# Three small layers beside a biased attention layer: the next causal one runs before the last gated one, and the order of all steps is new

## The chip, the core and the metric

The kernel runs on one core of a Trainium2 chip. Its time is the device time of one launch in microseconds (us), the median of several runs. The core has a matrix engine (PE in the profile, with its weight loads shown as PEld), a vector engine (DVE), a scalar engine (ACT), a general engine (POOL), a queue engine (SP) that issues the transfers, and eight accumulation banks, the tile `ps`, into which PE writes and out of which DVE and ACT read.

## What is computed

The input x is 8 samples of 512 tokens by 256 channels, in float32. Four layers follow each other, each with its own normalisation and a residual sum:

```python
x = x + attn_a(layernorm(x))   # causal: 16 heads of 16, rotary positions
x = x + ffn(layernorm(x))      # gated, l = 1: top half of the tokens by a gate, attention among them, scattered back
x = x + attn_b(layernorm(x))   # biased: 16 heads of 64, a table of 511 relative biases, index clamped
x = x + ffn(layernorm(x))      # gated, l = 3: the same function and weights as l = 1
```

In the causal layer the scores are masked above the diagonal; in the gated layers 256 of the 512 tokens are chosen by the rank of their gate, and the result is weighted by the gate. Samples do not depend on each other.

## The kernel before

All work is cut into steps, `Step(kind, s, l, n, q)`: `s` is the sample, `l` the layer (0 causal, 1 gated, 2 biased, 3 gated), `n` a head group or a pair of heads, `q` a part of it. The letter ahead of a kind is that of its layer, `c_`, `f_` or `b_`. There are 2256 steps; 1760 of them run on PE. `Plan(whole())` makes one list of them, and each engine walks that one list and does its own share of each step, so that the list is the order on every engine at once. PE never overtakes: a PE step that waits holds up all behind it.

The list is made in `in_order`. Among the steps whose predecessors have been placed it takes the one with the smallest `turn`, a number that `turn` reads from the table `PLACE` by kind, `n` and `q`, in rows for the first samples (`first0`, `first1`, `first`), the repeated middle (`cycle`, `cycle3`) and the end (`last`, `last1`, `last2`); `CYCLE` times the sample is added in the middle. `whole()` gives the predecessors: the data that a step needs, and what must be placed ahead of it because memory is shared.

The program has this shape. Samples 0 and 1 start with their causal and first gated layers, with little to run beside them. Then come eight biased layers, one per sample, each of them the frame of a cycle: beside the biased layer of sample s run three small layers, and they run one after another in one shared place of memory (`side`, `place_of` 0): the last gated layer of sample s-1, then the causal layer of s+1, then the first gated layer of s+1. The last gated layer of sample 7 stands alone at the end. Cycles for s = 2 to 6 have the same order.

The steps that matter below:

- `b_k`, `b_q`, `b_v` are projections of a pair of heads (L960 in PE's rows), `b_row` a 128-row block of scores (L1691), `b_nrm` its division on POOL (L1133), `b_tr` its transposition (L1699), `b_val` its product with the values (L1709), `b_y` the output projection (L1470).
- `c_xt` transposes the normalised input (L1501), `c_q` and `c_k` project it (L960); DVE, POOL and ACT then rotate it and split it into a high and a low part (`c_dq`, `c_rq`, `c_xq`, `c_dk`, `c_hk`). `c_p1` (L1529) computes scores for the row maxima, which DVE takes (L1325); `c_p2` (L1553) computes them again, transposed and with the maximum taken off, and ACT takes their exponentials (L1198); `c_va` and `c_vb` are the products with the values.
- `f_q`, `f_k`, `f_v` are projections; `f_p1` (L1624) and `f_p2` (L1646) are the gated counterparts, read by DVE (L1399) and ACT (L1205). `f_hm` and `f_m` turn the maxima between them, `f_va` and `f_vb` (L1658) multiply with the values, `f_o` and `f_y` (L1470) end the layer.
- `c_p1`, `c_p2`, `f_p1` and `f_p2` each take four of the eight banks, and use PE in pieces of 32 rows. `b_row` uses 64 rows, `b_val` 64 columns, the value products of the small layers 32 columns, everything else the whole array. The column `32*128` or `128*64` in PE's rows is this cut.
- Where `in_order` expects PE to wait, it has idle transpositions put ahead of the step (L1490, `ps<-ident`), called fillers here: 653 matmuls in all. They compute nothing that is used.
- `load_rope` reloads two tables of 256 KB each (`cos`, `sin`) ahead of each causal layer, since a gated layer has overwritten them. SP issues it after the last `f_vb` of the gated layer that ran last in the place.

Of the kernel before, what the change touches and what calls it, by code (L numbers as in the profile page):

```python
# [187 lines left out]
def wait_for(x, y):  # L188
# [7 lines left out]
    if x.kind == "f_spread" and y.kind == "f_rank":  # L196
# [7 lines left out]
    ("cycle", "b_k"): [3518, 1169, 1334, 4006, 4463, -33303, 4684, 5254],  # L204
    ("cycle", "b_ln"): [-15605],
    ("cycle", "b_nrm"): [1730, 3640, 2810, 3176, -4032, 3806, 3306, 4094, 4046, 4157, 4200, 4231, -9958, 4064, -3484,
        -36992, 4582, -9960, 3649, 4846, -48934, 1082, -48936, 5309, -36527, 3182, 5174, 5565, -49123, 4685, 5627,
        5511],
    ("cycle", "b_q"): [1785, 979, -3985, 4186, -35860, -37112, 8, -13072],
    ("cycle", "b_row"): [3590, 761, 3095, 3597, -13675, 3728, 2692, 1528, 993, 4334, 4077, 3578, 4077, 4040, 3589,  # L210
        -9153, 4509, -35108, -9630, 4077, -35254, 5214, -32634, -12835, -37081, 5135, 3041, 5508, 5529, 5511, 5563,
        5383],
    ("cycle", "b_tr"): [3656, 3997, -9445, 4075, 3460, 4272, 4094, 3973, 4077, -34795, 4410, -37079, -9958, -9958,
        4065, 4504, 5008, 5131, 4114, -9717, -36997, 5317, -11276, 5429, 4877, 5442, 5681, -12901, 5249, 5696, 5264,
        4627],
    ("cycle", "b_v"): [2758, 3587, 4079, 4385, -71, 4805, -48961, -1478],
    ("cycle", "b_val"): [4352, -9978, 4104, 4067, -33729, 3381, 3714, 1132, 4591, -41659, -33412, 3315, -37187, 4670,
        4115, 3613, 5428, 3980, -9596, 4938, 5509, -1425, -32633, 5575, 5738, 5511, 5950, 5980, 6159, 4292, 6176,
        5511],
    ("cycle", "b_xt"): [3459],  # L220
    ("cycle", "b_y"): [6233, 6258, 5177, 6270],
    ("cycle", "c_dk"): [-1887, 1803],
    ("cycle", "c_dq"): [-7637, 1401],
    ("cycle", "c_hk"): [-38074, -40051],
    ("cycle", "c_hm"): [1885, 2367],
    ("cycle", "c_k"): [-10624, 1724],
    ("cycle", "c_ln"): [1401],
    ("cycle", "c_m"): [1174, -51742],
# [199 lines left out]
    ("last2", "f_spread"): [2866],  # L428
    ("last2", "f_v"): [22412],
    ("last2", "f_va"): [34817, 38087],  # L430
    ("last2", "f_vb"): [19123, 7896],
    ("last2", "f_xq"): [17183],
    ("last2", "f_y"): [41504, 5562],
}
# [1345 lines left out]
```

## Time and profile before

| what | value |
|---|---|
| median of 3 runs | 2064.11 us (2063.27 to 2064.46) |
| the profiled execution, whole | 2061.41 us |
| its span, first to last instruction | 2059.7 us |
| PE busy in the span | 1988.9 us (97%) |
| DVE, ACT, POOL busy | 1516.3, 1152.8, 692.5 us (74%, 56%, 34%) |
| transfers, 16 engines | 14.6% of their time, 50 GB/s |
| share of PE on the chain that ended last | 76% |

The page has the busy time of each engine and, in 40 slices of the span, the tenths of a slice in which it was busy. The timeline lists runs of equal instructions with their start; the distance from one row's start to the next row's start is what a step costs PE. PE's own durations overlap, since matmuls are pipelined. A matmul in plain float32 counts twice there.

### The profile page before, as it was taken

The page shows a single profiled execution, that of the slowest core. Times are in us where ns is not written, and L with a number is a line of the kernel's source. Part 1 is how long each engine was busy: PE and PEld are TensorE (multiplying, and loading weights), DVE is VectorE, ACT ScalarE, POOL GpSimd, SP SyncE. Part 2 cuts the span into 40 slices and gives each one's busy share as a digit, 9 for nine tenths or more (in the row PEclk, how much of TensorE's full clock was granted, in tenths as well). Part 3 has the DMA queues.
Part 4 walks back from the last instruction along what each step waited for, and adds up shares of the span by engine and source line. Part 5 has one row for each costly group of instructions (what it writes and reads, how often), then busy time and mean ns, then how long its engine had stood idle before and what let it go on. Part 6 is the DMA issues. An engine that isn't in the chain of part 4 may idle for free.

```text
span 2059.7 us, 42179 instructions
## 1 busy us (share of the span) xinstructions
PE 1988.9 (97%) x16097; PEld 1282.8 (62%) x16097; DVE 1516.3 (74%) x4803; ACT 1152.8 (56%) x2578; POOL 692.5 (34%) x879
## 2 busy tenths in 40 slices
PE   8999999999999999999999999999999999999998
PEld 6676666655666556765566655665566655675667
DVE  8977654967868767778778687686876967857446
ACT  2535764756637475374755657466573756627742
POOL 5323232343414433234423343234341343413320
PEclk9999999999999999999999999999999999999999
DMA  4001121120102211121111211012110120102200
GB/s 166 2 1 35 52 77 45 61 98 17 63 16 73 73 35 44 34 80 55 35 37 52 83 42 45 19 59 83 35 63 2 60 90 17 63 16 70 70 1 22
DMA packets 31079, 102.46 MB, mean 50 GB/s; under 512 B 3104, under 2 KB 11424, under 8 KB 30752
## 3 DMA queue, kind: packets, MB, share of 16 engines
q1 hardware_dynamic: 30880, 99.76, 14.6%
q8 instruction: 130, 2.13, 0.4%
q14 instruction: 69, 0.57, 0.1%
HBM read 95.56 MB, written 4.19 MB: 48 GB/s over the span
## 4 chain that ended last, share of the span: by engine, by line
PE 76%; DVE 12%; ACT 5%; POOL 3%; issue 2%; DVEq 0%; POOLq 0%
PE ps L960 18%; PE ps L1709 11%; PE ps L1691 11%; PE ps L1699 10%; PE ps L1470 9%; ACT PTc L1198 3%; PE ps L1553 3%; PE ps L1658 3%; PE ps L1646 3%; PE ps L1567 3%; DVE ps L1325 2%; PE ps L1529 2%; DVE peaks L1399 2%; DVE probs L1416 2%; PE ps L1624 1%
## 5 line engine op out<-in xcount | busy, mean ns | idle before, releaser
L1133 POOL TENSOR_SCALAR probs<-probs,rtotal 128x512 f32<-128x512 f32 x512 | 345.9, 695 | 513.2 <-DVE rtotal L1425 512.3
L1225 ACT ACTIVATE probs<-probs,peak 128x512 f32<-128x512 f32 x512 | 365.3, 715 | 134.2 <-DVE peak L1421 133.3
L1416 DVE CUSTOM_DVE_ANT_0 probs<-ps,band 128x512 f32<-128x512 f32 x512 | 332.7, 687 | 60.6 <-PE ps L1691 60.2
L1234 ACT ACTIVATE PT<-ps 128x512 f32<-128x512 f32 x512 | 261.5, 620 | 52.5 <-PE ps L1699 52.1
L1699 PE MATMUL ps<-ident,probs 128*128 128x128 f32 x2048 | 245.3, 274 | 3.6 <-DVE peaks L1399 2.2
L1325 DVE CUSTOM_DVE_ANT_0 ps<-ps,later 128x512 f32<-128x512 f32 (+3 forms) x512 | 232.6, 526 | 20.3 <-PE ps L1529 20.0
L1691 PE MATMUL ps<-KT,QT 64*128 64x512 f32 x1024 | 243.8, 607 | 0.0
L1699 PEld LDWEIGHTS ps<-ident,probs 128*128 128x128 f32 x2048 | 225.2, 141 | 29.2 <-POOL probs L1133 12.0
L1709 PE MATMUL ps<-PT,Vb 128*64 128x512 f32 x1024 | 237.0, 600 | 0.0
L960 PE MATMUL ps<-xnT,wb 128*128 128x512 f32 x512 | 233.4, 600 | 0.6 <-ACT xnT L1158 0.6
L1198 ACT ACTIVATE PTc<-ps 128x384 f32<-128x384 f32 (+1 forms) x384 | 168.2, 549 | 42.4 <-PE ps L1553 41.4
L1399 DVE TENSOR_REDUCE peaks<-ps 128x2 f32<-128x512 f32 x256 | 157.2, 682 | 22.2 <-PE ps L1624 22.2
L960 PEld LDWEIGHTS ps<-xnT,wb 128*128 128x128 f32 x512 | 93.6, 190 | 113.1 <-issue 107.0
L1125 POOL TENSOR_SCALAR_AFFINE_SELECT PTc<-PTc 128x512 f32<-128x512 f32 x128 | 81.5, 649 | 233.8 <-ACT PTc L1198 233.4
L1096 POOL TENSOR_TENSOR rstd<-veps,pow_half 128x2 f32<-128x2 f32 x64 | 46.5, 731 | 329.8 <-DVE veps L1256 329.8
L1691 PEld LDWEIGHTS ps<-KT,QT 64*128 64x128 f32 x1024 | 94.8, 186 | 91.6 <-issue 67.2
L1205 ACT ACTIVATE PTf<-ps 128x512 f32<-128x512 f32 x256 | 131.3, 646 | 34.0 <-PE ps L1646 34.0
L1709 PEld LDWEIGHTS ps<-PT,Vb 128*64 128x64 f32 x1024 | 66.6, 136 | 129.1 <-issue 117.0
L960 PEld LDWEIGHTS ps<-wb,xnT 128*128 128x128 f32 x1024 | 121.2, 192 | 24.6 <-issue 22.7
L960 PE MATMUL ps<-wb,xnT 128*128 128x128 f32 x1024 | 127.3, 278 | 0.0
L1470 PE MATMUL ps<-wob,OTb 128*128 128x256 f32 x512 | 113.7, 379 | 0.0
L1470 PEld LDWEIGHTS ps<-wob,OTb 128*128 128x128 f32 x512 | 96.6, 190 | 12.4
(156 smaller groups left out, 3343.0 us busy)
## 6 DMA issues: line engine op xcount, KB each, us to landing
band<-in_band SPq DMA_DIRECT2D x64, 896.0 KB, 4.6
wb<-in_w_b SPq DMA_DIRECT2D x64, 384.0 KB, 3.1
x<-in_x SPq DMA_DIRECT2D x16, 256.0 KB, 3.0
out<-x SPq DMA_DIRECT2D x16, 256.0 KB, 2.2
cos<-in_cos SPq DMA_DIRECT2D x8, 256.0 KB, 2.7
sin<-in_sin SPq DMA_DIRECT2D x8, 256.0 KB, 2.9
wob<-in_wo_b SPq DMA_DIRECT2D x1, 1024.0 KB, 8.6
wqk<-in_wqk_a SPq DMA_DIRECT2D x1, 512.0 KB, 5.8
```

The lines of the kernel that those rows point to most:

```text
L960: last = nc.tensor.matmul(o, w, r, start=(i == 0), stop=(i == len(pairs) - 1))
L1133: last = g.tensor_scalar(unit, unit, rtotal[:, r % 8, e:e + 1], 1.0, ALU.mult, ALU.mult)
L1198: a.activation(pt_c(m, q)[:, h], bank(now, name)[:, 0:w], ACT.Exp, scale=float(DH) ** -0.5).then_inc(act_read, 1)
L1225: last = a.activation(unit, unit, ACT.Exp, bias=peak[:, r % 8, e:e + 1], accum_out=total[:, r % 8, e:e + 1])
L1234: a.activation(PT[:, k % 2, e, :, tile_of(q)], bank(now, name).rearrange("p (k n) -> p k n", k=NT), ACT.Copy).then_inc(act_read, 1)
L1325: last = v.tensor_tensor_reduce(out=scores, in0=scores, in1=later[:, NT * P - w:NT * P], scale=1.0, scalar=-3e38, op0=ALU.add, op1=ALU.max ...
L1399: v.tensor_reduce(places[:, h:h + 1].rearrange("p h t -> p (h t)"), bank(now, name).rearrange("p (t n) -> p t n", t=NS), AXIS.X, ALU.max). ...
L1416: v.tensor_tensor_reduce(out=probs[:, r % ROWS_HELD, e, :], in0=bank(now, name), in1=band[:, k % 2, e, lo:lo + T], scale=1.0, scalar=-3e38 ...
L1470: last = te.matmul(o[:, j * D:(j + 1) * D], w, r, start=(k == 0 and j == 0), stop=(k == count - 1 and j == 1))
L1691: full(te.matmul(bank(now, name), QT2[half(e), k % 2, tile_of(q)], KT2[half(e), k % 2, :], start=True, stop=True), now, name)
L1699: last = te.transpose(bank(now, name)[:, tile_of(t)], probs[:, r % ROWS_HELD, e, tile_of(t)], ident[:])
L1709: last = te.matmul(o[half(e), :], Vb[:, k % 3, q, half(e)], PT[:, k % 2, e, q, :], start=(q == 0), stop=(q == NT - 1))
```

## The change

The three small layers beside a biased layer change places: first the causal layer of s+1, then the last gated layer of s-1, then the first gated layer of s+1. They still follow each other in the shared place. The condition for the rotary tables moves with it: they are reloaded after the last `f_vb` of the first gated layer, not of the last one. All numbers of `PLACE` are replaced, in the rows of the start and of the end too. No step is added or removed, and no operation of a step is changed.

```diff
@@ causal_steps
-    turned = [Step("f_vb", s - 2, 3, 1)] if s >= 2 else []
-    out = [(c("ln"), late, [Step("f_part", s - 2, 3)] if s >= 2 else []), (c("xt"), [c("ln")], side)]
+    turned = [Step("f_vb", s - 1, 1, 1)] if s >= 2 else []
+    out = [(c("ln"), late, [Step("f_part", s - 1, 1)] if s >= 2 else []), (c("xt"), [c("ln")], side)]
@@ whole
         if s > 0:
-            gone = add(ffn_steps(s - 1, 3), left, side)
-            side = gone
+            turned = []
             if s + 1 < B:
-                side = add(ffn_steps(s + 1, 1), add(causal_steps(s + 1, side), [], []), [])
+                turned = add(causal_steps(s + 1, side), [], [])
+            side = add(ffn_steps(s - 1, 3), left, turned + side)
+            if s + 1 < B:
+                side = add(ffn_steps(s + 1, 1), turned, side)
                 entered.append(side)
@@ block.sync
-                        if kind == "f_vb" and l == 3 and n == 1 and s + 2 < B:
+                        if kind == "f_vb" and l == 1 and n == 1 and 1 <= s < B - 1:
                             sp.wait_ge(heads_done, plan.after("heads", now, now))
-                            load_rope(sp, s + 2)
+                            load_rope(sp, s + 1)
@@ PLACE
-    ("cycle", "c_ln"): [1401],
...
-    ("cycle", "f_y"): [3437, 2898],
```

Lines after the table have numbers smaller by four in the changed kernel (L1470 is L1466 there, L1490 is L1486).

First place: PE, where a causal layer starts in a middle cycle. `xn` is the normalised input under transposition, `xnTc` the causal layer's transposed input, `xnT` the biased layer's, `wob` the weights of `b_y`. Before:

```order
L1470 MATMUL ps<-of_lo_143,spread_t_140 128x256 x2
L1501 MATMUL ps<-ident,xn 128x128 x8
L1490 MATMUL ps<-ident 128x128 x6
L960 MATMUL ps<-xnTc_106,wqk 128x512 x6
L960 MATMUL ps<-xnT,wb 128x512 x8
L960 MATMUL ps<-wb,xnT 128x128 x8
L1529 MATMUL ps<-LO_100,X_96 128x128 x4
```

Now:

```order
L1466 MATMUL ps<-of_lo_143,spread_t_140 128x256 x2
L1497 MATMUL ps<-ident,xn 128x128 x8
L1466 MATMUL ps<-wob,OTb 128x256 x8
L956 MATMUL ps<-xnTc_106,wqk 128x512 x2
L1497 MATMUL ps<-ident,xn 128x128 x8
L956 MATMUL ps<-xnTc_106,wqk 128x512 x6
L956 MATMUL ps<-xnT,wb 128x512 x4
L1466 MATMUL ps<-wob,OTb 128x256 x16
```

Six fillers stood between the transposition and the projections of the causal layer; now half of a `b_y` stands there, and the next biased layer's transposition lies between two of the projections. Behind the last projection of the causal layer nine steps of the biased layer follow before the first `c_p1` (2 `b_k`, 2 `b_q`, 2 parts of `b_y`, 3 `b_row`), where five projections of it did.

Second place: PE, in the last part of the first gated layer of a middle cycle (the rows of L1646 are one `f_p2` in two halves, then come the value products with `PTf` and `Vx`). Before:

```order
L1646 MATMUL ps<-gX_123,gLO_125 128x256 x4
L1646 MATMUL ps<-gX_123,gHI_124 128x256 x4
L1646 MATMUL ps<-gM_127,sel 128x256 x4
L1709 MATMUL ps<-PT,Vb 64x512 x4
L1658 MATMUL ps<-PTf_129,Vx 32x256 x16
L1709 MATMUL ps<-PT,Vb 64x512 x4
L1470 MATMUL ps<-wof,OTf_139 128x256 x4
```

Now:

```order
L1642 MATMUL ps<-gX_123,gLO_125 128x256 x4
L1642 MATMUL ps<-gX_123,gHI_124 128x256 x4
L1642 MATMUL ps<-gM_127,sel 128x256 x4
L1654 MATMUL ps<-PTf_129,Vx 32x256 x8
L1486 MATMUL ps<-ident 128x128 x5
L1654 MATMUL ps<-PTf_129,Vx 32x256 x8
L1705 MATMUL ps<-PT,Vb 64x512 x4
L1466 MATMUL ps<-wof,OTf_139 128x256 x4
```

Half of a `b_val` between the last `f_p2` and the value products is gone from there; five fillers have come between the two value products.

Third place: PE, in the same layer, from its projections to its first `f_p1` (L1624). Before:

```order
L1709 MATMUL ps<-PT,Vb 64x512 x2
L960 MATMUL ps<-xgT_141,wkf 128x256 x4
L960 MATMUL ps<-xgT_141,wqf 128x256 x4
L960 MATMUL ps<-wvf,xgT_141 128x256 x4
L1699 MATMUL ps<-ident,probs 128x128 x24
L1624 MATMUL ps<-gLO_125,gX_123 128x256 x4
```

Now:

```order
L956 MATMUL ps<-xgT_141,wqf 128x256 x4
L956 MATMUL ps<-xgT_141,wkf 128x256 x4
L956 MATMUL ps<-wvf,xgT_141 128x256 x4
L1695 MATMUL ps<-ident,probs 128x128 x32
L1620 MATMUL ps<-gLO_125,gX_123 128x256 x4
L1620 MATMUL ps<-gHI_124,gX_123 128x256 x4
```

One more `b_tr` (8 transpositions) stands between, and the projection of q comes ahead of that of k.

## Rows read from the trace of the kernel before

**Rows 1.** The page: busy time by engine, and PE and its clock in 40 slices.

```profile
PE 1988.9 (97%) x16097; PEld 1282.8 (62%) x16097; DVE 1516.3 (74%) x4803; ACT 1152.8 (56%) x2578; POOL 692.5 (34%) x879
...
PE   8999999999999999999999999999999999999998
...
PEclk9999999999999999999999999999999999999999
```

**Rows 2.** Busy time by stretch: the start, one middle cycle, the end; columns in the first line.

```profile
core 0: us, PE busy (x) PEld busy (x) DVE busy (x) ACT busy (x) POOL busy (x), PEclk, DMA share, GB/s
0.00:180.00 180.00, 164.86 (x1747) 116.30 (x1748) 151.31 (x495) 71.64 (x148) 66.31 (x83) 1.00 0.14 49
...
840.10:1087.20 247.10, 239.75 (x1940) 151.95 (x1939) 188.59 (x601) 143.93 (x322) 86.33 (x108) 1.00 0.15 50
...
1832.60:2059.70 227.10, 216.75 (x1616) 147.75 (x1614) 132.08 (x390) 115.53 (x262) 56.43 (x75) 1.00 0.12 40
```

**Rows 3.** The fillers alone (L1490), same stretches: length, PE busy, PEld busy.

```profile
0.00:180.00 180.00, 50.50 (x382) 41.41 (x382) 1.00 0.14 49
...
840.10:1087.20 247.10, 1.58 (x11) 1.21 (x11) 1.00 0.15 50
...
1832.60:2059.70 227.10, 24.99 (x199) 21.95 (x199) 1.00 0.12 40
```

**Rows 4.** Timeline of PE at the start: start, length, instruction, idle before.

```profile
start us, us, engine line op out<-in xcount [idle before <-releaser]
...
101.13 6.33 PE L1490 MATMUL ps<-ident 128*128 128x128 f32 x56
108.45 0.65 PE L1580 MATMUL ps<-ident,gate 128*128 128x128 f32 x4 [1.00 <-DVE gate L1364]
108.94 3.44 PE L1490 MATMUL ps<-ident 128*128 128x128 f32 x30
114.06 0.18 PE L960 MATMUL ps<-ones,tie 128*128 128x1 bf16 x1 [1.68 <-DVE above L1374]
```

**Rows 5.** Timeline of PE: a run of eight b_val parts.

```profile
905.85 7.09 PE L1709 MATMUL ps<-PT,Vb 128*64 128x512 f32 x32
912.87 1.97 PE L1699 MATMUL ps<-ident,probs 128*128 128x128 f32 x16
```

**Rows 6.** Timeline of PE: a single b_val part between two other cuts.

```profile
1058.89 1.08 PE L1709 MATMUL ps<-PT,Vb 128*64 128x512 f32 x4
1059.90 0.39 PE L1646 MATMUL ps<-gX,gLO 32*128 32x256 f32 x4
```

**Rows 7.** Timeline of PE where the causal layer of a middle cycle starts.

```profile
926.58 1.03 PE L1501 MATMUL ps<-ident,xn 128*128 128x128 f32 x8
927.45 0.82 PE L1490 MATMUL ps<-ident 128*128 128x128 f32 x6
928.57 5.42 PE L960 MATMUL ps<-xnTc,wqk 128*128 128x512 f32 x12 [0.30 <-ACT xnTc L1158]
...
943.52 0.33 PE L1529 MATMUL ps<-LO,X 32*128 32x128 f32 x4 [0.88 <-POOL LO L1118]
```

**Rows 8.** Timeline of PE at the first f_p1 of the first gated layer.

```profile
1046.35 2.78 PE L1699 MATMUL ps<-ident,probs 128*128 128x128 f32 x24
1050.13 0.39 PE L1624 MATMUL ps<-gLO,gX 32*128 32x256 f32 x4 [0.99 <-issue]
...
1051.72 3.23 PE L1699 MATMUL ps<-ident,probs 128*128 128x128 f32 x24 [0.36 <-DVE peaks L1399]
```

**Rows 9.** Timeline of PE in that layer's last part.

```profile
1067.50 1.94 PE L1709 MATMUL ps<-PT,Vb 128*64 128x512 f32 x8
1069.37 1.93 PE L1658 MATMUL ps<-PTf,Vx 128*32 128x256 f32 x32
```

**Rows 10.** Timeline of ACT in the same part: exponentials of two f_p2.

```profile
1065.68 4.03 ACT L1205 ACTIVATE PTf<-ps 128x512 f32<-128x512 f32 x8 [0.43 <-PE ps L1646]
```

**Rows 11.** Timeline of PE: two steps that each wait for four banks.

```profile
979.65 0.39 PE L1553 MATMUL ps<-X,LO 32*128 32x256 f32 x4 [0.35 <-DVE peaks L1325]
...
981.30 0.45 PE L1529 MATMUL ps<-LO,X 32*128 32x384 f32 x4 [0.74 <-ACT PTc L1198]
```

**Rows 12.** The page: DVE's reads of one f_p1 bank each.

```profile
L1399 DVE TENSOR_REDUCE peaks<-ps 128x2 f32<-128x512 f32 x256 | 157.2, 682 | 22.2 <-PE ps L1624 22.2
```

More of the change, by code:

```diff
@@ L419 @@
-    ("last2", "f_m"): [25353, 3866],
-    ("last2", "f_o"): [39842],
-    ("last2", "f_p1"): [22427, 21766, 23453, 12693],
-    ("last2", "f_p2"): [33553, 33746, 4835, -13],
-    ("last2", "f_part"): [2865],
-    ("last2", "f_q"): [1858],
-    ("last2", "f_rank"): [14396],
-    ("last2", "f_row"): [3077],
-    ("last2", "f_rq"): [-4341],
[L428 to L432, printed above, removed]
@@ new lines @@
+    ("cycle", "f_k"): [513],
+    ("cycle", "f_ln"): [-11359],
+    ("cycle", "f_m"): [851, -10902],
+    ("cycle", "f_o"): [1046],
+    ("cycle", "f_p1"): [-11995, -12175, 950, 826],
+    ("cycle", "f_p2"): [979, 1028, -11306, -11702],
+    ("cycle", "f_part"): [342],
+    ("cycle", "f_q"): [511],
+    ("cycle", "f_rank"): [419],
+    ("cycle", "f_row"): [110],
+    ("cycle", "f_rq"): [-13073],
+    ("cycle", "f_spread"): [462],
+    ("cycle", "f_v"): [534],
+    ("cycle", "f_va"): [1031, -10391],
@@ new lines @@
+    ("cycle", "f_vb"): [-10725, -11738],
+    ("cycle", "f_xq"): [756],
+    ("cycle", "f_y"): [1065, -11187],
+    ("cycle3", "f_gate"): [5082],
+    ("cycle3", "f_gather"): [5156],
+    ("cycle3", "f_hk"): [5470],
+    ("cycle3", "f_hm"): [-6566, 5566],
+    ("cycle3", "f_k"): [5239],
+    ("cycle3", "f_ln"): [2551],
+    ("cycle3", "f_m"): [5473, 5677],
+    ("cycle3", "f_o"): [5759],
+    ("cycle3", "f_p1"): [-5262, -5202, 5624, 5498],
+    ("cycle3", "f_p2"): [5568, 5635, -7238, -5135],
+    ("cycle3", "f_part"): [2999],
@@ new lines @@
+    ("first1", "f_p2"): [3188, 3257, 3228, 3221],
+    ("first1", "f_part"): [-1180],
+    ("first1", "f_q"): [2560],
+    ("first1", "f_rank"): [1665],
+    ("first1", "f_row"): [-1089],
+    ("first1", "f_rq"): [-1954],
+    ("first1", "f_spread"): [3135],
+    ("first1", "f_v"): [3174],
+    ("first1", "f_va"): [3304, 3383],
+    ("first1", "f_vb"): [3272, 3198],
+    ("first1", "f_xq"): [2763],
+    ("first1", "f_y"): [3668, 3334],
+    ("last", "b_k"): [8902, 7787, 7336, 8369, 7335, 10602, 17154, 19458],
@@ new lines @@
+    ("last", "b_xt"): [22230],
+    ("last", "b_y"): [30878, 17289, 21678, 12362],
+    ("last1", "f_gate"): [21886],
+    ("last1", "f_gather"): [17330],
+    ("last1", "f_hk"): [17965],
+    ("last1", "f_hm"): [-4908, -2944],
+    ("last1", "f_k"): [-3695],
+    ("last1", "f_ln"): [17972],
+    ("last1", "f_m"): [17287, 17970],
+    ("last1", "f_o"): [17344],
+    ("last1", "f_p1"): [-6750, -4747, 17345, 17103],
+    ("last1", "f_p2"): [17222, 17353, 17663, 16629],
+    ("last1", "f_part"): [17972],
@@ new lines @@
+    ("last2", "f_ln"): [7455],
+    ("last2", "f_m"): [20850, 21215],
+    ("last2", "f_o"): [23953],
+    ("last2", "f_p1"): [6518, 20503, 20687, 20749],
+    ("last2", "f_p2"): [7727, 6965, 1405, 11083],
+    ("last2", "f_part"): [6686],
+    ("last2", "f_q"): [5471],
+    ("last2", "f_rank"): [19307],
+    ("last2", "f_row"): [4964],
+    ("last2", "f_rq"): [5746],
+    ("last2", "f_spread"): [19687],
+    ("last2", "f_v"): [10260],
+    ("last2", "f_va"): [22340, 22868],
+    ("last2", "f_vb"): [7932, 7392],
@@ L434 @@
+    ("last2", "f_xq"): [20231],
+    ("last2", "f_y"): [25246, 16616],
 }
```

368 lines of the change are left out of this document (154 added, 214 removed).

## The prediction

> **What bounds the kernel now.** I read the page first. PE is busy for 97% of the span and DVE, the next, for 74%; of the 40 slices only the first and the last are below nine tenths, and the granted clock is full (2.4 GHz, the upper of its two levels) in all of them [rows 1]. So PE sets the end, and a new order can only change three things on it: what it pays when it changes between cuts of the array, how long it waits for data or banks, and how long it stands under fillers. The work itself is the same 1760 steps.
>
> The stretches say where waits are. The first 180 us have 382 fillers and 15 us of idle; the last 227 us have 199 fillers; a middle cycle is 247.1 us long, with 7.4 us of idle (247.10 - 239.75) and 11 fillers [rows 2, 3]. The cycle repeats within 0.1 us, so one stands for the others. In it DVE is busy for 188.6 us, 76%, ACT and POOL for less [rows 2]: no other engine can set its length, though each can be late for a moment. Transfers are busy for 15% of their time.
>
> **Changes of cut.** Counting neighbours in the order of PE with different cuts gives 718 changes before and 694 now: 4 fewer in each cycle from s = 1 to 6, 4 fewer in the stretch ahead of it, 4 more in the last cycle. Their price: eight parts of `b_val` in a row take 7.02 us from start to start (905.85 to 912.87), of which about 0.15 is the way in and out, so 0.86 each [rows 5]. One part alone between other cuts takes 1.01 us (1058.89 to 1059.90) [rows 6]. The difference, 0.15 us, is one way in and one way out, which is one change. 24 x 0.15 = **3.6 us less**. From below nothing excludes 0.1, from above 0.2 (other pairs of cuts may cost more): 2.4 to 4.8.
>
> **Fillers at the start and the end.** In the order, samples 0 and 1 have 418 fillers after, 382 before, and the last layer 203 after, 193 before. What stands under them is a wait. A stretch of 56 took 7.32 us (101.13 to 108.45), which is 0.13 each; one of 30 took 5.12 us (108.94 to 114.06), 0.17 each, with 1.68 us of idle behind it [rows 4]. I take 0.15: 36 x 0.15 = 5.4 us more at the start and, of 10 x 0.15 = 1.5, two thirds at the end, since the 30 fillers at the same place were already too few to fill the wait and 40 will partly fill what was idle. Together **6.4 us more**. The lower end is 0: fillers fill time, they need not make it, and the waits they stand for could have been idle before at places that carry none. The upper end is 46 x 0.17 = 7.8. I stay near the upper end because PE does nothing else there: the one wait of 71 fillers in the new order, ahead of the first `f_row`, was one of 56.
>
> **The middle cycle, place by place.** Gains first.
> - The causal layer's transposition was followed by fillers and idle, 1.12 us (927.45 to 928.57) [rows 7]. Now half a `b_y` stands there, longer than the wait. 1.1 less.
> - The first `c_p1` waited 0.88 us for POOL [rows 7], with five projections behind the causal layer's own. Nine steps stand there now, nearly twice the time. 0.9 less.
> - The first `f_p1` of the first gated layer waited 0.99 us [rows 8]. One more `b_tr` stands ahead; from one of three in a run of 24, that is 0.9 us, and `f_q` comes first, whose way over DVE, ACT and DVE is the long one. I take 0.6 less, since its banks are read a little later.
>
> Then losses.
> - The last `f_p2` of that layer had half a `b_val` behind it (1.87 us, 1067.50 to 1069.37) before the two value products began [rows 9]. ACT needed 4.03 us for eight exponentials and finished at 1069.71 [rows 10]. Without the half the first value product begins at 1067.5, the second 0.97 later, and the second needs the last of these exponentials: 1069.7 + 0.1 - 1068.5 is 1.3, with the handover about 1.4. The order has five fillers at just that place. 1.4 more.
> - `f_m` 1 stood behind its last `f_p1` by 3.3 us of work, now by 2.6 (one `f_p2`, half a `b_val`). DVE's four reads are 4 x 0.68 = 2.7 us [rows 12], and two small copies follow. 0.5 more.
> - Steps with four banks that follow each other directly wait 0.35 and 0.74 us [rows 11]. Each order has such a run in its causal layer (then `c_p2`, `c_p1`, now `c_p1`, `c_p1`), so I let them cancel. The five fillers at the `c_p2` parts stay too, at the neighbouring step.
>
> The reload of the rotary tables (two transfers of 256 KB) now goes out about 14 us of PE work before the causal layer's first projection (`b_val`, `f_o`, `b_y`, `f_y`, `c_xt`, `b_y`); what SP has queued behind it, the loads of bands and weights for pairs two further on, waits only for that one `f_vb`. I cost it at nothing; if the tables came late, `c_k` 0 would stand, once a cycle, for the excess.
>
> The cycle's sum is -1.1 - 0.9 - 0.6 + 1.4 + 0.5 = -0.7; small waits elsewhere I cannot price from places that do not exist yet. For six cycles **4.2 us less**, between 14 less (2.3 each) and 6 more (1.0 each).
>
> **The sum.** -3.6 + 6.4 - 4.2 = -1.4 against the profiled execution's 2061.41 us, or 2060.0. That execution lies 2.70 us below the median of the runs (2064.11), so the same step from the median gives 2062.7; I say **2062.5 us**. A measurement of this kernel can tell about 0.2% from no change, which is 4.1 us, so this counts as no change.
>
> **Rivals.**
> - *The middle gains more.* A whole layer now stands between the causal layer of a sample and its gated one, so neither has to wait for the other's tail, and the three gains come in full while the small waits of four-bank steps shrink with them. 2.3 us less per cycle is 13.8; with -3.6 and +6.4 that is -11.0: 2053. For it speaks that DVE's 76% leaves room; against it, that 7.4 us of idle in a cycle is all there is to win in plain sight and most of it is at four-bank steps, of which there are as many as before.
> - *The start costs nothing.* The added fillers stand in time that was idle anyway. -3.6 + 1.0 - 4.2 = -6.8: 2057. Against it: of the 15 us of idle at the start only a part lies behind fillers [rows 2, 4].
> - *Slower: the banks' readers become the bound in the small layers' dense parts.* Neighbouring steps that take four banks each are 98 in the new order and 90 before, and the end of the first gated layer has lost its cover. ACT needs 4.03 us for two `f_p2` [rows 10], PE 1.9 us for a step and a value product, so any lateness of ACT goes on through the run. If the tail costs 2.4 instead of 1.4 and the runs of `c_p1` another 0.7, the cycle is 1.0 longer: +6.0 - 3.6 + 6.4 = +8.8: 2073. It decides as soon as the tail and the runs cost over 0.7 us a cycle more than I gave them. The Trainium skill says something near this (TensorEngine Tiling (Array Packing), PSUM Bottleneck): a cut array speeds up PE but not the reading of its banks, which may then be the bottleneck. By that rule alone each of the 8 added neighbours would cost the excess of reading over filling.
> - *The change doesn't do what it says.* The three layers still share one place and still exclude each other, and PE was busy through all their borders, so the swap as such may do nothing, and only the new table counts. This is inside the forecast.
>
> **How the numbers follow.** The forecast, with its own range of 2058 to 2068, gets 0.44, of which 0.07 lies below 2060; the middle gains more 0.20; the start costs nothing 0.14; slower 0.22, all but a little beyond 2068.2. So faster by over 0.2%: 0.41; within: 0.37; slower: 0.22. To leave out no more than 2 in 10 the range reaches to both outer cases but not over them: 2051 to 2072.
>
> **What the profile after would show.** Steps right: a cycle of about 245.8 us (247.1 - 0.7 - 0.6); no fillers and no idle before `c_q` and none before the first `c_p1`; about 1.4 us with five fillers before the second value product of the first gated layer; some 5 us more under fillers in the first 180 us; DVE, ACT and POOL as busy as before. Wrong: idle of over 1 us at a `c_p1` or `f_p2` where none was (slower), a cycle below 244.5 us (the first rival), the start no longer than before (the second), or PE waiting at `c_k` for a transfer. The clock should stay full in every slice; if it fell anywhere, all this would be beside the point.

## The result, and the profile after

The changed kernel takes **2072.08 us** (median of 6 runs, 2071.0 to 2072.75); the kernel before, run beside it on the same chip, 2064.28 (2062.92 to 2064.68). The ratio is 1.0039 [1.0026, 1.0052]. So it is slower by 7.8 us and lies 0.08 us above the predicted range (2051 to 2072), where 2062.5 and "no change" had been forecast. The profiled execution took 2071.28 us with a span of 2069.6, against 2061.41 and 2059.7 before: 9.9 us more in the spans. The 7.8 us between the medians are the better measure of the change: about 2 of the 9.9 come from the clock of the two executions that were profiled (see the paragraph on the clock below).

The page of the changed kernel, against [rows 1], shows PE busy for 10 us longer with the same work and the same share, and the other engines within 5 us of before:

```profile
PE 1999.2 (97%) x16137; PEld 1291.8 (62%) x16137; DVE 1520.9 (73%) x4803; ACT 1157.0 (56%) x2578; POOL 695.6 (34%) x879
```

A share says nothing here of where 10 us went. The stretches do. These are the windows of the changed kernel, from one `b_xt` to the next (length, then PE, PEld, DVE, ACT, POOL busy, granted clock, transfers): the start, the cycle of s = 1, one middle cycle, the end.

```profile
core 0: us, PE busy (x) PEld busy (x) DVE busy (x) ACT busy (x) POOL busy (x), PEclk, DMA share, GB/s
0.00:181.50 181.50, 165.90 (x1757) 117.37 (x1757) 148.06 (x487) 71.95 (x148) 65.46 (x83) 0.99 0.14 49
...
334.30:603.70 269.40, 259.18 (x2023) 163.65 (x2022) 195.28 (x619) 146.29 (x325) 88.42 (x110) 0.99 0.15 47
...
850.40:1097.50 247.10, 240.04 (x1939) 152.27 (x1938) 189.20 (x601) 144.57 (x322) 86.88 (x108) 1.00 0.15 50
...
1842.40:2069.60 227.20, 217.53 (x1626) 147.99 (x1624) 131.67 (x390) 115.41 (x262) 56.61 (x75) 1.00 0.12 40
```

The middle cycle and the end are as long as in [rows 2]: 247.1 and 227.2 us, before 247.1 and 227.1. The start is 1.5 us longer. What stands out is the cycle of s = 1, 269.4 us. That stretch was not among the rows that I had picked for the prediction; in the kernel before it is

```profile
335.40:593.00 257.60, 250.25 (x1990) 161.21 (x1989) 191.08 (x607) 143.96 (x322) 86.39 (x108) 1.00 0.15 48
```

To split this I took each PE step's distance to the start of the next one, called the shortest distance among its repeats (with the same change of cut) its work, and the rest a wait:

| stretch | length, before / after | work | under fillers | waits |
|---|---|---|---|---|
| up to `b_xt` of s = 0 | 180.0 / 181.5 | -3.5 | +2.9 | +2.2 |
| s = 0 | 155.4 / 152.8 | -3.6 | +0.4 | +0.5 |
| s = 1 | 257.6 / 269.4 | +5.1 | +1.1 | +5.6 |
| s = 2 to 6 together | 1239.6 / 1238.7 | -2.1 | 0.0 | +1.4 |
| s = 7 and the end | 227.1 / 227.2 | +0.8 | +0.6 | -1.4 |
| all | 2059.7 / 2069.6 | -3.3 | +4.9 | +8.3 |

Steps that moved across a border show as work there; only the sum of that column is a gain. (Rows and columns add up within 0.2 us.) The lengths and the column of the fillers can be read directly. The line between work and waits can't be drawn so sharply in the dense part: with the lower tenth or the lower quarter of the repeats in place of the shortest, or with the cut of the step ahead counted too, the same two traces give -8 to +4 us of work for s = 2 to 6, 4 to 7 for s = 1 and -10 to +4 for all, with the waits the other way. Only the sum of the two columns is firm there. By `b_xt` of s = 2 the new kernel is 10.7 us late, and at the end 9.9.

**What stands at the entry of s = 1.** The timeline of PE in the changed kernel (start, length, instruction, idle before):

```profile
334.32 1.04 PE L1497 MATMUL ps<-ident,xn 128*128 128x128 f32 x8
338.46 0.66 PE L1497 MATMUL ps<-ident,xn 128*128 128x128 f32 x4 [3.11 <-DVE xn L1259]
339.46 0.66 PE L1497 MATMUL ps<-ident,xn 128*128 128x128 f32 x4 [0.34 <-DVE xn L1259]
339.95 1.26 PE L1486 MATMUL ps<-ident 128*128 128x128 f32 x6
341.07 8.37 PE L956 MATMUL ps<-xnTc,wqk 128*128 128x512 f32 x16
```

The first L1497 row is `b_xt` of sample 1, the next two are `c_xt` of sample 2. Between them PE stands still for 3.11 us and once more for 0.34. DVE's timeline tells why:

```profile
335.39 0.75 DVE L1245 BATCH_NORM_STATS2 stats<-x 128x6 f32<-128x256 f32 x2 [6.21 <-PE ps L1497]
...
338.66 0.74 DVE L1259 TENSOR_SCALAR xn<-x,mv,rstd 128x256 f32<-128x256 f32 x2 [0.26 <-POOL rstd L1092]
```

The normalised input of every layer goes through one tile, `xn`. DVE may not begin the normalisation of sample 2 (`c_ln`) before PE has read that of sample 1 out of it; it had waited 6.21 us for that. Then PE waits for DVE's chain of 4 us, and there is nothing between. In the kernel before the same `b_xt` is followed by a run of a whole `b_y`:

```profile
335.43 1.09 PE L1501 MATMUL ps<-ident,xn 128*128 128x128 f32 x8
336.36 14.01 PE L1470 MATMUL ps<-wob,OTb 128*128 128x256 f32 x64
```

In the later cycles of the changed kernel `c_xt` comes ahead of `b_xt`, with half a `b_y` and a `c_k` between them, so there is no such wait. It can occur only once, in the first cycle that has the new sequence. Right behind it `c_k` takes 8.37 us for its 16 matmuls. The granted clock there, and in a first window from the start of the kernel (it is the column behind the busy times):

```profile
114.90:118.30 3.40, 3.29 (x16) 2.93 (x20) 3.40 (x20) 0.00 (x0) 0.00 (x0) 0.50 0.00 0
336.80:340.20 3.40, 1.40 (x11) 1.17 (x12) 2.27 (x9) 0.27 (x1) 1.40 (x2) 1.00 0.06 22
340.20:343.60 3.40, 3.40 (x9) 1.78 (x7) 0.00 (x0) 0.81 (x2) 0.00 (x0) 0.50 0.00 0
343.60:347.00 3.40, 3.40 (x9) 1.52 (x8) 2.24 (x6) 0.00 (x0) 1.23 (x1) 1.00 0.02 5
```

After a stretch in which PE was busy for 1.40 of 3.40 us the clock was at its lower level, 1.2 GHz, for 3.4 us, and then full again. The first row is the other such stretch, near 115. It is not the new order's doing: kernels 2 and 7 below, which start in the order of the kernel before, have one there too (from 115.9 and from 116.3), and kernel 5, with the same start, has none.

**The middle places that I had priced.** The first `c_p1` (873.06) and, behind `c_xt` and half a `b_y`, the first `c_k` (1095.80) start without idle; the first `f_p1` (1061.21) still waits for 0.70 us, and the two last value products of the first gated layer stand apart (compare [rows 7, 8, 9]):

```profile
873.06 0.33 PE L1525 MATMUL ps<-LO,X 32*128 32x128 f32 x4
...
1061.21 0.39 PE L1620 MATMUL ps<-gLO,gX 32*128 32x256 f32 x4 [0.70 <-issue]
...
1079.21 1.07 PE L1654 MATMUL ps<-PTf,Vx 128*32 128x256 f32 x16
1080.22 0.77 PE L1486 MATMUL ps<-ident 128*128 128x128 f32 x5
1081.40 1.07 PE L1654 MATMUL ps<-PTf,Vx 128*32 128x256 f32 x16 [0.41 <-ACT PTf L1201]
...
1091.47 1.03 PE L1497 MATMUL ps<-ident,xn 128*128 128x128 f32 x8
1092.34 3.62 PE L1466 MATMUL ps<-wob,OTb 128*128 128x256 f32 x16
1095.80 1.88 PE L956 MATMUL ps<-xnTc,wqk 128*128 128x512 f32 x4
```

### The profile page after: what moved, and what is told of

Read it like the earlier page. It is cut to its first block, busy times and chain, and to the rows that moved or that the text cites. A ratio compares the mean times of both kernels' runs of the same rounds, so it can differ in the third digit from the quotient of the medians.

```text
span 2069.6 us, 42217 instructions
## 1 busy us (share of the span) xinstructions
PE 1999.2 (97%) x16137; PEld 1291.8 (62%) x16137; DVE 1520.9 (73%) x4803; ACT 1157.0 (56%) x2578; POOL 695.6 (34%) x879
## 4 chain that ended last, share of the span: by engine, by line
PE 72%; DVE 18%; ACT 6%; issue 2%; POOL 2%; DMA 0%; SPq 0%; DVEq 0%; POOLq 0%
PE ps L956 22%; PE ps L1466 10%; PE ps L1687 9%; PE ps L1695 8%; PE ps L1705 7%; DVE ps L1321 4%; DVE probs L1412 4%; PE ps L1549 3%; DVE peaks L1395 3%; PE ps L1642 3%; ACT PTc L1194 3%; ACT PTf L1201 2%; PE ps L1654 2%; PE ps L1525 1%; PE ps L1486 1%
## 5 line engine op out<-in xcount | busy, mean ns | idle before, releaser
L1687 PEld LDWEIGHTS ps<-KT,QT 64*128 64x128 f32 x1024 | 99.6, 186 | 95.3 <-issue 72.9
L1466 PE MATMUL ps<-wob,OTb 128*128 128x256 f32 x512 | 113.6, 379 | 0.0
L1466 PEld LDWEIGHTS ps<-wob,OTb 128*128 128x128 f32 x512 | 96.7, 190 | 14.9 <-issue 2.4
```

The source lines that it names most:

```text
L1466: last = te.matmul(o[:, j * D:(j + 1) * D], w, r, start=(k == 0 and j == 0), stop=(k == count - 1 and j == 1))
L1687: full(te.matmul(bank(now, name), QT2[half(e), k % 2, tile_of(q)], KT2[half(e), k % 2, :], start=True, stop=True), now, name)
```

## Experiments

Theory A: the hand-over of `xn` at the entry costs about 5 us of the loss. Theory C: the new order of the start costs the other 4 to 5. The rivals were that the middle cycles or the tail of the first gated layer carry it, and that the swap itself does. "Medians" below are set beside the kernel before in the same group of runs: 2063.90 for the first four, 2062.99 for the next four, 2062.46 for the next two and 2063.09 for the last.

### 1. A tile of its own for the normalised input of sample 2

The steps that write and read `xn` now ask `xn_of` which tile to take.

```diff
+        xn_own = over(side[0], 2048, "xn_own", [P, NT, D])
+        def xn_of(step):
+            return xn_own if step.kind in ("c_ln", "c_xt") and step.s == 2 else xn
...
-                            if old is not None and old.kind == "f_part":
+                            if kind == "c_ln" and s == 2:
+                                pass
+                            elif old is not None and old.kind == "f_part":
```

> The changed kernel, in which the normalised input of sample 2's causal layer gets a buffer of its own, so that its normalisation (c_ln) need not wait until PE has transposed the biased layer of sample 1 out of the shared buffer xn. Nothing else differs, and the order is the same. Theory A (the loss is this one hand-over of xn at the start of the cycle of s = 1, where PE idles 3.11 and 0.34 us in front of c_xt, stands 1.1 us under fillers and then runs 1.3 us longer at half clock): the idle goes, the granted clock stays full there, and the kernel is 4 to 6 us faster than the changed one, about 2067. Theory B (the causal layer's start is late for any reason, and the wait returns at the first c_p1 behind it): the idle in front of c_xt goes but as much appears before the first c_p1 of sample 2, and the time stays at 2072. Theory C (the start of the program alone holds the loss): no change.

Measured: 2066.91 us, ratio 1.0017 [1.0008, 1.0027]. Its timeline of PE at the entry:

```profile
335.08 1.04 PE L1505 MATMUL ps<-ident,xn 128*128 128x128 f32 x8
335.95 1.04 PE L1505 MATMUL ps<-ident,xn_own 128*128 128x128 f32 x8
336.82 0.82 PE L1494 MATMUL ps<-ident 128*128 128x128 f32 x6
338.05 7.13 PE L962 MATMUL ps<-xnTc,wqk 128*128 128x512 f32 x16 [0.41 <-ACT xnTc L1160]
```

The same order of steps, the waits gone, `c_k` back at 7.13 us, and the cycle of s = 1 at 264.3 us instead of 269.4. Of these 5.1 us, 3.45 are the two waits and 1.24 (8.37 - 7.13) is the clock. Theory A holds.

### 2. The old order up to the first `b_xt`

```diff
+    order = in_order(whole(B), places=PLACE_OLD)[0]
+    order = order[:order.index(Step("b_xt", 0, 2))]
+    order += [x for x in in_order(whole(1))[0] if x not in set(order)]
```

> The changed kernel, with the order of the kernel before up to the transposition of the first biased layer (b_xt of sample 0), and the new order behind it. Theory C (the loss is in the start: 5.1 us more of waits and fillers in the first 180 us, against 3.5 us less of work placed there): the first biased layer starts at 180.0 instead of 181.5 with more done, the start of the biased layer of sample 1 comes some 6 us earlier than 334.3, and the kernel is 5 to 7 us faster than the changed one, about 2066. Theory A alone (all of the loss at the hand-over in the cycle of s = 1): no gain from this, 2072, and the idle in front of c_xt is still there at the start of that cycle. If both hold, this gains its part and the idle in front of c_xt stays as it was.

Measured: 2067.58 us, ratio 1.0018 [1.0008, 1.0028]. `b_xt` of s = 1 comes at 329.6 us instead of 334.3, so 4.7 us were in the start, and the hand-over is untouched:

```profile
329.64 1.04 PE L1752 MATMUL ps<-ident,xn 128*128 128x128 f32 x8
333.79 0.66 PE L1752 MATMUL ps<-ident,xn 128*128 128x128 f32 x4 [3.10 <-DVE xn L1514]
```

Theory C holds too, for its part.

### 3. Work in the gap: four parts of `b_val`

```diff
+def moved(order):
+    some = [Step("b_val", 0, 2, 6, q) for q in range(4)]
+    return put(order, some, Step("c_xt", 2, 0))
```

> The changed kernel, with four parts of one b_val (3.4 us of PE work of sample 0, from behind the projections) put between b_xt of sample 1 and c_xt of sample 2. Theory A (an uncovered wait, to be had back by putting any work over it): the idle of 3.11 us goes, the clock stays full, 4 to 5 us faster, 2067. Theory B (work as cover is only moved: what covers one wait uncovers another): the wait for the first c_p1 of sample 2, which the same b_val covered, comes up instead; 1 to 3 us faster at most, 2069 to 2071.

Measured: 2069.38 us, ratio 1.0023 [1.0014, 1.0033]. The gap is filled:

```profile
335.51 3.65 PE L1720 MATMUL ps<-PT,Vb 128*64 128x512 f32 x16
339.10 1.25 PE L1512 MATMUL ps<-ident,xn 128*128 128x128 f32 x8
...
361.74 0.76 PE L1501 MATMUL ps<-ident 128*128 128x128 f32 x5
```

The cycle of s = 1 is 265.7 us, 3.7 shorter, where the own tile gave 5.1. Work taken from elsewhere covers the wait, but its old place loses it: ahead of the first `c_p1` of sample 2, where this `b_val` had stood, 0.86 us under fillers have come up (361.74 to 362.60).

### 4. Fillers in the gap

Twenty-eight unused transpositions stand ahead of this `c_xt`; all else is as in the changed kernel.

```diff
+                        if kind == "c_xt" and s == 2:
+                            room(now, "o")
+                            for i in range(28):
+                                te.transpose(bank(now, "o")[:, tile_of(i % NT)], ident[:], ident[:])
```

> The changed kernel, with 28 fillers (3.1 us of transpositions that nothing uses) in front of c_xt of sample 2, where PE idles 3.11 us and after which its granted clock is half for 3.4 us. Nothing waits for less. If the lower clock follows from PE having idled there, it stays full, the first projections behind take 7.2 us instead of 8.4, and the kernel is 1 to 1.3 us faster, 2071. If the clock falls for another reason it falls again, and the time is 2072 or a little more.

Measured: 2072.05 us, ratio 1.0034 [1.0021, 1.0048]. Locally the clock part comes back: the cycle of s = 1 is 268.0 us, 1.4 shorter, with the clock full at the place where it had been half. But in this execution it was half elsewhere, for 6.8 us near 113 and for 3.4 near 1895:

```profile
340.20:343.60 3.40, 3.10 (x15) 1.83 (x14) 0.05 (x2) 1.09 (x2) 0.00 (x0) 1.00 0.02 5
1891.20:1894.60 3.40, 1.87 (x43) 1.36 (x39) 3.26 (x8) 1.60 (x5) 0.00 (x0) 1.00 0.39 116
1894.60:1898.00 3.40, 3.40 (x30) 1.89 (x24) 0.09 (x1) 3.34 (x8) 0.00 (x0) 0.50 0.00 0
```

A gain of 1 us can't be told in the medians (ratios 1.0034 and 1.0039, each with an interval of over 0.1% either way). That the clock stayed up at 340 under the fillers is seen in one execution, and kernel 7 below shows that it can stay up there without them. Ahead of the fall near 1895 PE had been busy for 1.87 of 3.40 us, with two waits for DVE of 0.79 and 0.74 us; the changed kernel has the same two waits (0.81 and 0.73, near 1894), and its profiled execution had no fall there.

### 5. Both repairs

The own tile of 1, the start of 2 and the table's old rows for the end; from the cycle of s = 1 on, the swapped sequence with its new numbers.

> Three parts together: the old order up to the first biased layer's transposition, the own buffer for the normalised input of sample 2's causal layer, and the old numbers for the last cycle and the end; the middle cycles keep the swapped order. From the two runs of one part each: start 4.7 us, hand-over of xn 5.1 us, and the end by 10 fillers fewer about 1 us, together 10 to 11 us less than the changed kernel's 2072.1, so 2061 to 2062, 1 to 3 us under the kernel before. If instead the two parts saved the same time twice (both act on when the biased layer of sample 1 gets going), it stays at 2065 to 2067.

Measured: 2063.50 us, ratio 1.0003 [0.9994, 1.0013], span 2060.3. The whole loss is gone, and nothing more. Its cycles from s = 2 to 6 take 1238.5 us, 1.1 less than before. In the whole it stands 1.5 us longer under fillers than the kernel before and gets 0.9 of it back in work and waits together; how these two share it isn't shown, for the reason given at the table. This speaks against the middle cycles as the cause, and leaves no gain for the swap.

### 6. The tail of the first gated layer covered again

Half a `b_val` of pair 7 goes back to its old place behind the last `f_p2`, ahead of the last two value products, in the six cycles from s = 1.

```diff
+    for s in range(1, B - 1):
+        some = [Step("b_val", s, 2, 7, q) for q in range(2)]
+        order = put(order, some, Step("f_va", s + 1, 1, 1))
```

> The changed kernel, with the half b_val of the tail put back where it stood before, in the cycles of s = 1 to 6: behind the last f_p2 of the first gated layer and ahead of its value products. Theory D (the prediction's step: the uncovered tail costs a cycle 1.4 us, and covering it gives that back): 1.2 to 1.8 us less a cycle, 7 to 10 us in all, 2063 to 2065. Theory E (the half stood ahead of f_m 1, where it covered DVE's reads of f_p1; a cover can be moved but not won): the wait under the fillers goes and one of the same size comes up at f_m 1; within 3 us of 2072, either way.

Measured: 2074.84 us, ratio 1.0054 [1.0040, 1.0068]. The 1.18 us ahead of the second value product (1080.22 to 1081.40 above) are gone, but where the `b_val` had stood, ahead of `f_m` 1 (L1646), there are now fillers and idle:

```profile
1073.09 1.20 PE L1503 MATMUL ps<-ident 128*128 128x128 f32 x9
1075.24 0.44 PE L1646 MATMUL ps<-ident,peaks 128*128 128x128 f32 x2 [0.94 <-ACT PTf L1218]
...
1082.58 1.93 PE L1671 MATMUL ps<-PTf,Vx 128*32 128x256 f32 x32
```

From 1073.09 to 1075.24 are 2.15 us. The five cycles from s = 2 take 1240.2 us instead of 1238.7, 0.3 more each. The cover was moved, and nothing was won. The rest of the difference in the spans (2074.0 to 2069.6) is the start, the entry and the end, where this execution had the clock at half for 6.8, 6.8 and 3.4 us.

### 7. The swap only from the cycle of s = 2

The order of before up to and with `b_xt` of s = 2, and the new sequence behind it.

```diff
-    order = order[:order.index(Step("b_xt", 0, 2))]
+    order = order[:order.index(Step("b_xt", 2, 2)) + 1]
```

> The old order and structure through the cycle of s = 1 and b_xt of sample 2, the swapped ones from there on. Theory F (the first swapped cycle pays an entry, wherever it is: its c_ln is placed behind b_xt and waits for xn, since no earlier cycle has drawn it forward): b_xt of sample 2 starts at 593.0 as in the kernel before, PE idles 3 us or more in front of c_xt of sample 3, the cycle of s = 2 is 250 us or longer, and the later ones 246.9; in all 5 to 8 us slower than before, 2069 to 2072. Theory G (the hand-over cost is peculiar to the cycle of s = 1, where much is left over from sample 0): the cycle of s = 2 is 247 us like the others, and the kernel is within 1.5 us of the kernel before.

Measured: 2070.32 us, ratio 1.0034 [1.0022, 1.0047]. `b_xt` of s = 1 comes at 337.2, of s = 2 at 594.7. The hand-over appears one cycle later, to the hundredth of a microsecond:

```profile
594.70 1.04 PE L1752 MATMUL ps<-ident,xn 128*128 128x128 f32 x8
598.85 0.66 PE L1752 MATMUL ps<-ident,xn 128*128 128x128 f32 x4 [3.11 <-DVE xn L1514]
```

That cycle takes 253.5 us where the next takes 247.1. Of the 6.4 more, 3.45 are the two waits; 28 fillers instead of 10 stand in it too (4.1 us of PE, where the 11 of [rows 3] took 1.6). So the price belongs to the border between the two sequences, not to sample 1 or 2.

### 8 and 9. The swap with the old numbers, and the new numbers without the swap

> The swap alone: the layers change places and the reload of the tables moves, with all the old numbers of the kernel before. Theory H (the swap by itself gains or costs little, since PE is busy through the layers' borders): a middle cycle of 245 to 252 us and 2055 to 2100 in all. Theory I (the numbers carry the overlap; with the old ones each small layer is taken up late and PE waits with nothing beside it): middle cycles longer by tens of us, 2200 or more, at the same busy times of DVE, ACT and POOL.

> The other half of the pair that the kernel with the swap and the old numbers began: the steps and their needs as in the kernel before (old last gated layer, new causal layer, new first gated layer), with the new table PLACE. The order then has 1897 fillers, 693 with the swap and the same table. THEORY I (the numbers carry the overlap, and they fit only the sequence of layers they were found for): much slower, by at least the 1204 more fillers at 0.13 us or 157 us, and with idle behind them as in the other half (there 784 more fillers came with 249 us): 2250 to 2450. RIVAL (the swap alone makes the loss, the numbers are interchangeable): about 2064 to 2072.

Measured, one run each: 2322.74 and 2363.66 us. One middle cycle of either, the swap with the old numbers first:

```profile
930.10:1220.20 290.10, 263.20 (x2071) 171.47 (x2070) 188.52 (x601) 144.31 (x322) 86.12 (x108) 0.98 0.13 43
```

```profile
940.20:1238.20 298.00, 272.40 (x2141) 178.59 (x2140) 189.99 (x601) 145.35 (x322) 87.10 (x108) 0.96 0.12 42
```

The cycle grows from 247 us to 290 and 298, with 142 and 211 fillers in it instead of 10 or 11, while DVE, ACT and POOL do what they always do. The two halves of the change make sense only together, so its effect can't be split into "swap" and "numbers"; what can be split is the start, the border and the middle.

### 10. A better order

The kernel of 5, with many steps moved by a few places (in the cycles from s = 2 to 6 by the same places), chosen to shorten the waits.

```diff
+        ranks = {x: i + SHIFTS.get((x.kind, x.l, x.n, x.q), {}).get(x.s, 0) for i, x in enumerate(want)}
+        self.order, banks_of, self.spare = in_order(steps, ranks)
```

> The swap with the own buffer at the entry, the start and the end of before, and many steps of the rest moved by a few places each (the same move in each cycle from s = 2 to 6, others at the start and in the cycle of s = 1). Beside the kernel with both repairs (2063.5 us) the order has 630 fillers instead of 653 (12 fewer at the start, 10 fewer in the cycle of s = 1) and 700 changes of cut instead of 691. THEORY J (the swapped sequence has gain left that its numbers did not reach): fillers 23 x 0.13 = 3.0 less, changes of cut 9 x 0.15 = 1.4 more, some waits in the cycle of s = 1 gone with its fillers, 1 to 4 us: 2058 to 2062, a middle cycle below 246.5. THEORY K (cover is moved, not won: each wait taken away comes up at a neighbour): 2062 to 2066, a middle cycle of 246.9 as before the moves.

Measured: 2057.35 us (7 runs, 2055.65 to 2059.1), ratio **0.9974 [0.9962, 0.9985]**: faster than both kernels. Its start, and one middle cycle:

```profile
0.00:175.00 175.00, 164.68 (x1735) 116.48 (x1736) 149.64 (x495) 71.82 (x148) 66.52 (x83) 1.00 0.14 50
1087.20:1334.50 247.30, 239.74 (x1940) 152.17 (x1939) 187.97 (x600) 144.76 (x322) 86.00 (x109) 1.00 0.15 50
```

In the kernel of 5 the start was 180.3 us and such a cycle 246.9. So theory J is right only in its total: the gain is in the start. From there to the end this kernel takes 1880.6 us and that of 5 1880.0. In the middle theory K's number came out: the moves of steps there won nothing.

### 11. The same start under the kernel before

```diff
+        start = [Step(*x) for x in START]
+        want = start + [x for x in in_order(steps)[0] if x not in set(start)]
+        self.order, banks_of, self.spare = in_order(steps, {x: i for i, x in enumerate(want)})
```

`START` lists the same 153 steps that stand there before, in the order of kernel 10.

> The kernel before, steps and table unchanged, with only its first 153 steps (all that stand ahead of the first b_xt) in the order that the improved one has; the rest follows in the order of before. THEORY L (the 5 us that the improved order gained over the kernel with both repairs lie in the start alone, where its b_xt of s = 0 came at 175.0 instead of 180.3, and have nothing to do with the swap): b_xt of s = 0 at 175 to 176, all later stretches as before (247.1 per cycle), 2057 to 2059. RIVAL M (the start only hands its wait on: what starts earlier in PE's order waits for DVE or ACT in the next stretch, which the moves in the cycle of s = 1 were needed to avoid): b_xt of s = 0 early, but s = 1 or s = 2 within 1 us of before, 2061 to 2064.

Measured: 2058.61 us (11 runs, 2056.06 to 2059.98), ratio 0.9978 [0.9969, 0.9987]. The stretches:

```profile
175.30:330.80 155.50, 154.89 (x1040) 94.74 (x1038) 98.50 (x312) 101.97 (x236) 51.07 (x72) 1.00 0.21 69
330.80:588.30 257.50, 250.13 (x1989) 160.98 (x1988) 191.06 (x607) 143.95 (x322) 86.54 (x108) 1.00 0.15 48
588.30:835.40 247.10, 239.73 (x1940) 151.76 (x1939) 188.62 (x601) 143.95 (x322) 86.56 (x108) 1.00 0.15 50
```

`b_xt` of s = 0 comes 4.7 us earlier, and every later stretch is as long as before; nothing is handed on. Theory L holds. A part of it can be read at the waits for the gate. Before, PE stood under 56 fillers and 1.00 us of idle there [rows 4]. Now:

```profile
100.15 6.01 PE L1528 MATMUL ps<-ident 128*128 128x128 f32 x53
106.00 0.60 PE L1618 MATMUL ps<-ident,gate 128*128 128x128 f32 x4
```

The gate's transposition comes at 106.00 instead of 108.45, with no idle ahead of it. The ratios of kernel 10 and of this one lie within each other's intervals, so with the same good start no difference is shown between the swapped sequence (with its own tile) and the old one.

## Why the prediction was wrong

**Right: PE sets the end, and only cuts, waits and fillers can change.** In every experiment DVE's, ACT's and POOL's busy times per cycle stayed within 2 us, while PE's length moved with its waits. Even in 8 and 9, 40 to 50 us longer per cycle, they did not change.

**Right in its sign, priced too high: the changes of cut.** Forecast 3.6 us less. The 0.15 came from a single `b_val` part of 1.01 us. Over both traces a part takes 0.86 us from start to start ahead of another and 0.96 ahead of a different cut (median of 372 and of 140), a `b_row` block 0.86 and 0.96, a `b_q` 1.72 and 1.81; behind an `f_p2` no difference is seen (0.91). So a change costs 0.10 us at most pairs of cuts and the 24 are worth 2.4 us at most, the lower end that I had given. The table's 3.3 less work can't confirm more, since that column depends on the choice of the shortest distance. The Trainium skill says near this that changing the tiling mode drains TensorE (TensorEngine Tiling (Array Packing), Key Properties); the sign agrees with these rows.

**About right, by the wrong place: the start.** Forecast 5.4 us more for the start. Up to `b_xt` of s = 1 there are 3.3 us more under fillers and 2.7 more of waits, 6.0 together, and exchanging the order of the start brought 4.7 back. But 30 more fillers stand there, not 36, since I had compared 418 for samples 0 and 1 with a count that left out the 6 fillers of the cycle of s = 0; and each cost 0.11 us, not 0.15. The run that I had named, 71 fillers for 56, was hardly longer:

```profile
98.81 7.92 PE L1486 MATMUL ps<-ident 128*128 128x128 f32 x71
106.68 0.65 PE L1576 MATMUL ps<-ident,gate 128*128 128x128 f32 x4
```

It is 7.87 us here and was 7.32 in [rows 4]. Part of the waits was the clock: it was at half for 3.4 us near 115. That part isn't the new order's: with the order of before, the stretch up to the first `b_xt` takes 181.7 us in kernel 7, with such a fall, and 180.3 in kernel 5, without one.

**The end was oversized.** Of the 1.0 us for ten more fillers nothing is left: 0.6 more under fillers, 0.8 more work, four added changes among it, 1.4 less waits. The lower bound of that term (fillers need not make time) was the right value.

**Failed: "the cycle repeats within 0.1 us, so one stands for the others".** That sentence was about the kernel before, and even there it holds only for three stretches: from `b_xt` to `b_xt` s = 1 to 6 take 257.6, 247.1, 247.1, 247.7, 247.1 and 250.6 us. I multiplied the middle by six, and so took the cycle of s = 1 for a middle one. It is the border at which the old sequence ends and the new begins: I gave it -0.7 us, and it has +6.7 in fillers and waits. Of these, 3.45 are the wait for `xn` and 1.24 the clock behind it (experiment 1); the other 2.0 were not located. The order could have shown it: it has `b_xt` and `c_xt` side by side there with no filler between, and both use one tile (DVE's chain between them took 4 us, 335.39 to 339.40). I had looked at the places that the middle had, and at totals of fillers; a wait for which the order holds no filler appears in neither, and this kernel never puts fillers ahead of a `c_xt`.

**Mis-sized: the middle.** With the changes of cut a cycle was to be 1.3 us shorter (-0.7 and -0.6, 245.8 us); the five from s = 2 are 0.9 shorter together, 0.2 each. Of the three gains two came in full (1.1 and 0.9), the third gave 0.3 instead of 0.6. The losses were 1.8 (1.18 at the last value product and 0.64 at two `f_p2` ahead of it) instead of 1.4, and 0.3 instead of 0.5. So the priced places give -0.2 instead of -0.7, and the changes of cut -0.4 at most instead of -0.6. The other 0.4 would lie in the small waits that I had put at nothing because I could not price them; it was not measured by itself. Experiment 6 shows for one wait that the work that covers it uncovers another, and in experiment 10 moving many steps did not shorten the middle cycle (247.3 us; 246.9 in kernel 5).

**The rivals.** The slower one, 2073 us, has the right size by luck and the wrong mechanism. (The range ended at 2072, 1 us below this rival's own figure.) It had the readers of the banks become late in dense runs for a full microsecond per cycle; the cycles from s = 2 to 6 are not longer at all. The total came from a place that no rival spoke of. "The middle gains more" and "the start costs nothing" are both refuted. "The change does nothing as such" is nearest to what kernels 10 and 11 show: with equal starts no difference between the two sequences is shown. The loads of the rotary tables, which I costed at nothing, cost nothing in a middle cycle: the first `c_k` starts without idle (1095.80).

**The clock.** I had written that a fall of the clock would put all else beside the point. It fell, but for 3.4 us at two places. The fall at `c_k` came behind the wait of the hand-over and took 1.24 us. It belonged in the sum as the price that a long wait can have, not in a reserve. The one near 115 also occurs in kernels 2 and 7 under the old order of the start, and PE's wait of 1.67 us for DVE ahead of it was 1.68 before [rows 4]. Such falls belong to both kernels: the profiled execution of the kernel before had none (mean granted clock 1.000), but of 66 other executions of it, beside kernels 1 to 11 (2060.8 to 2067.6 us), only 10 show 1.000. These average 2061.4 us, the 17 with 0.998, the value of the changed kernel's profiled execution, 2063.7. So the pair of profiled executions makes the change look about 2 us dearer than it is; at 0.998 the changed kernel (2071.0 and 2071.28) is 7.5 us slower.

## What to carry to other kernels

Where a change puts a new repeating pattern in place of an old one, cost three things apart: the pattern, the ends, and the border where one turns into the other; at the border, check each tile that both sides share, and let no repeated cycle stand for it. Adding up fillers finds the waits that were foreseen; the unforeseen one of this case stood where two steps with a dependency through another engine are neighbours and nothing is between them. In this kernel, whose main engine is busy for 97%, moving covers in the dense middle won nothing (experiments 6 and 10), and the time was to be had where the engine stands under fillers: a new order of 153 steps at the start gave 4.5 us, which all the moves in the rest did not.

## What the runs showed of the hardware

- A wait of 3.11 us, with the shorter one behind it, was followed by the loss of PE's full clock for 3.4 us in a kernel that is otherwise dense: 16 matmuls of 512 columns took 8.37 us instead of 7.13. In kernels 2 and 6 a wait of 3.10 us there was followed by a fall too, for 3.4 and 6.8 us. In kernel 7, with the wait of 3.11 us, there was none, and the 16 took 7.13:

```profile
601.45 7.13 PE L1210 MATMUL ps<-xnTc,wqk 128*128 128x512 f32 x16 [0.30 <-ACT xnTc L1409]
```

  So the same wait is followed by a fall in some executions and not in others. The Trainium skill (TensorE: Matmul & The Clock Gate, Part 1) says of the warm-up at a kernel's start that the number of matmuls at the lower clock varies between runs of one kernel. The rows here are of later falls, in the middle of a kernel.
- Such falls also come behind shorter waits. Ahead of the one near 1895 in kernel 4 PE was busy for 1.87 of 3.40 us (row above). Ahead of one near 2010 in kernel 10 it was busy for 1.73, with a wait of 1.67 us for DVE; at half clock it was then busy all the time:

```profile
2007.20:2010.60 3.40, 1.73 (x31) 1.39 (x30) 2.62 (x11) 0.00 (x0) 0.00 (x0) 1.00 0.00 0
2010.60:2014.00 3.40, 3.40 (x18) 3.40 (x17) 3.12 (x8) 0.00 (x0) 0.00 (x0) 0.50 0.00 0
```

  Kernels 5 and 11 each had one at the same steps (from 2015.8 and 2011.2). The profiled execution of the kernel before, with the same steps there and a wait of 1.62 us, had none. What decides it stays open.
- From the last `b_xt` to the end take 228.7 us in kernels 4, 5, 10 and 11, with one such fall, and 227.1 in the kernel before and in kernel 7, without. So a fall is worth 1.6 us there. The 66 executions named above rise with it, from 2061.4 us at a mean granted clock of 1.000 to 2067.0 at 0.996 (5 of them): the clock is a good part of the scatter between the runs of one kernel.
